# A bf16 copy of Wq and Wo in DRAM, made once at the start and read instead of casting loads

## The chip, the cores and the metric

One Trainium2 chip, one program on 8 cores. Each core works on its own half of one of four sequences and exchanges nothing with the others. The metric is device time in microseconds of the slowest core.

## What is computed

The reference is a transformer layer with a gate on its output: a layer norm, causal attention with 32 query heads and 8 key/value heads and a rotary embedding, and a low-rank mixture whose SiLU multiplies the attention's output.

```python
xn = _layernorm(x, axis=-1)                       # x: (4, 4096, 4096) float32
s = _L0_attn_ref(xn, Wq, Wk, Wv, Wo)              # q,k,v = xn @ W; rope; softmax(q k^T) v; out @ Wo
g = _silu(_L0_ffn_ref(xn, A, B, Wr, br))          # router softmax, low = xn A, out = low B * scores
x = x + s * g
return x
```

Wq and Wo are 4096 x 4096, Wk and Wv 4096 x 1024, all float32 in DRAM.

## The kernel before

The kernel keeps everything transposed: features on the partitions, 512 tokens across. It multiplies in bf16. Weights lie in DRAM in float32 and are converted by the DMA that loads them. Such a casting load is issued on POOL's queue (`load_wcol`, line 339): it brings one slab, 128 columns of a weight, into a tile of 128 x 4096 bf16 (1 MB). In DRAM a slab is 4096 runs of 512 bytes; in the tile each becomes 256 bytes.

There are two phases.

**First phase** (lines 470 to 566). Eight blocks of 512 tokens. For each, `p1_load` brings the 4 MB block of x (POOL's queue, casting, into XB0 or XB1 in turn) and `p1_stats` normalises it. Then for each of 8 key/value heads one slab of Wk and one of Wv are multiplied with the block (lines 496 and 535), K gets its rotary embedding, V is transposed, and both are stored to DRAM scratch (`kfs`, `vts`, on SP's queue). Two pairs of weight buffers take turns, so all 16 slabs of Wk and Wv are loaded again for every block.

**Second phase** (from line 570). Four slots of 512 query tokens, whose keys and values are 32, 24, 16 and 8 tiles long (`TRIPS`). In each slot:

- for each of 8 groups of four heads: four query projections (line 600, one slab of Wq each, 32 multiplications), the rotary embedding, norms for the softmax's bound, then the attention of the four heads (lines 697 to 747). Slab h+3 of Wq is loaded into one of three buffers wq0 to wq2 as soon as head h's projection is done (line 612). The keys and values of the next group come from kfs and vts on SP's queue (lines 678 and 681).
- the router and the low-rank gate (up to line 874),
- the output stage (lines 882 to 916): 32 chunks of 128 output features. Chunk `nck` multiplies its slab of Wo (three buffers, wo0 to wo2) with the attention's output: 32 multiplications, line 893. DVE multiplies the sum with the gate (line 908) and adds the residual tile xf (line 911), and SP stores it to `yqT` (line 914). The slab of chunk nck+3 is loaded when chunk nck is done (line 901). The residual tiles use two buffers, so the tile of chunk nck+1 (line 904) waits for the store of chunk nck-1.
- the setup of the next slot: sines, masks, its block of x, its layer norm.

The order on each engine is the order of the code. A small scheduler (`Sched`) works out for each instruction which semaphore counts it waits for, from the names of what it reads and writes. Every DMA takes the next of a fixed set of semaphore lanes, 4 on POOL and 6 on SP, and waits until that lane's last DMA has landed. So at most 4 DMAs of POOL and 6 of SP are in flight, and an engine that waits holds up all that stands behind it.

Of the kernel before, what the change touches and what calls it, by code (L numbers as in the profile page):

```python
# [11 lines left out]
BF16 = mybir.dt.bfloat16  # L12
# [9 lines left out]
NKV = 8  # L22
NH = 32
TW = 512
NTB = S // TW
NCD = D // 128
# [127 lines left out]
def build_program(dbg=False):  # L154
    nc = bass.Bass("TRN2", target_bir_lowering=False)
# [10 lines left out]
    Wq = din("Wq", [D, D])  # L166
    Wk = din("Wk", [D, KVD])
    Wv = din("Wv", [D, KVD])
    Wo = din("Wo", [D, D])
# [12 lines left out]
    constv = din("constv", [128, 12], F32)  # L182

    yqT = nc.dram_tensor("yqT", [D, NQ], F32, kind="ExternalOutput").ap()
    sk = "ExternalOutput" if dbg else "Internal"
    kfs = nc.dram_tensor("kfs", [NKV, 128, S], BF16, kind=sk).ap()
    vts = nc.dram_tensor("vts", [NKV, 128, S], BF16, kind=sk).ap()
# [11 lines left out]
    A = sch.add  # L199

    with ExitStack() as ctx:
        en = ctx.enter_context

        def sb(name, shape, dt):
# [15 lines left out]
        wq_sb = [sb(f"wq{i}", [128, NCD * 128], BF16) for i in range(3)]  # L220
        wo_sb = [sb(f"wo{i}", [128, NCD * 128], BF16) for i in range(3)]
# [78 lines left out]
                     writes=["cvt"], dma_sem="s_ld")  # L300
        for i, val in enumerate(CONST_VALS):
            nc.const_aps.register(F32, val, cvt[:, i:i + 1])
        for dst, nm, src in ((onec, "onec", ones_col), (oner, "oner", ones_row),
# [5 lines left out]
              writes=[nm], dma_sem="s_ld")  # L309
        A("gpsimd", lambda g: g.dma_start(  # L310
            out=a_sb[:].rearrange("p (c r) -> p c r", c=NCD),
            in_=Al.rearrange("(c p) r -> p c r", p=128)),
          writes=["a_sb"], dma_sem="s_cast")
        A("gpsimd", lambda g: g.dma_start(out=bm_sb[:], in_=Bml),
          writes=["bm_sb"], dma_sem="s_cast")

        A("tensor", lambda t: t.matmul(A0[:, 0:8], oner[:], brb[:], start=True, stop=True),
          reads=["oner", "brb"], writes=["A0"])
        A("vector", lambda v: v.tensor_copy(br_b[:], A0[:, 0:8]),
          reads=["A0"], writes=["br_b"])  # L320

        A("gpsimd", lambda g: g.dma_start(out=wr_bf, in_=Wr),
          writes=["XB0"], dma_sem="s_cast")
        for c in range(NCD):
# [3 lines left out]
              reads=["XB0", "idb"], writes=["D0"] if c == 0 else [])  # L328
        sch.mark_write("D0", "s_pe")
        A("vector", lambda v: v.tensor_copy(wrt[:], d0bf[:, 0:NCD * 8]),  # L330
          reads=["D0"], writes=["wrt"])

        def load_xblock(buf, bufname, src, col0):
            return A("gpsimd", lambda g: g.dma_start(
                out=buf[:].rearrange("p (c t) -> p c t", c=NCD),
                in_=src[:, col0:col0 + TW].rearrange("(c p) t -> p c t", p=128)),
                writes=[bufname], dma_sem="s_cast")

        def load_wcol(W, n0, buf, bufname):
            return A("gpsimd", lambda g: g.dma_start(  # L340
                out=buf[:].rearrange("p (c n) -> p c n", c=NCD),
                in_=W[:, n0:n0 + 128].rearrange("(c p) n -> p c n", p=128)),
                writes=[bufname], dma_sem="s_cast")

        def rep(ap2d, n, width):
            return ap2d.unsqueeze(1).to_broadcast([128, n, width])
# [111 lines left out]
        def p2_kv_load(slot):  # L458
# [5 lines left out]
                out=vtb[0][:, 0:T * 128], in_=vts[0][:, 0:T * 128]),  # L464
              reads=["vts.g0"], writes=[vtn[0]], dma_sem="s_ld")

        pending_vt = []
        p1_load(0)
        p1_stats(0)
# [4 lines left out]
        for tb in range(NTB):  # L474
# [4 lines left out]
            for g in range(NKV):  # L479
# [15 lines left out]
                for c in range(NCD):  # L495
# [4 lines left out]
                      reads=[wkn[gp], xname], writes=[PKn + ".lo"] if c == 0 else [])  # L500
                sch.mark_write(PKn + ".lo", "s_pe")
                A("vector", lambda v, gp=gp, PK=PK: v.tensor_copy(kraw[gp], PK[:, 0:512]),
                  reads=[PKn + ".lo"], writes=[krawn[gp]])
                A("tensor", lambda t, gp=gp, PK=PK: t.matmul(
                    PK[:, 512:1024], pib[:], kraw[gp], start=True, stop=True),
                  reads=[krawn[gp], "pib"], writes=[PKn + ".hi"])
                A("vector", lambda v, gp=gp, par=par: v.tensor_mul(
                    tmpA[:], kraw[gp], cosb[par][:]),
                  reads=[krawn[gp], f"cosb{par}"], writes=["tmpA"])
                A("vector", lambda v, par=par, PK=PK: v.tensor_mul(  # L510
                    tmpB[:], PK[:, 512:1024], sinb[par][:]),
                  reads=[PKn + ".hi", f"sinb{par}"], writes=["tmpB"])
                A("vector", lambda v, gp=gp: v.tensor_add(kout[gp], tmpA[:], tmpB[:]),
                  reads=["tmpA", "tmpB"], writes=[koutn[gp]])
                A("gpsimd", lambda gg, gp=gp: gg.tensor_mul(sqh, kout[gp], kout[gp]),
                  reads=[koutn[gp]], writes=["PP1.a"])
                A("tensor", lambda t: t.matmul(A0[0:1, :], onec[:], sqh,
                                               start=True, stop=True),
                  reads=["PP1.a", "onec"], writes=["A0"])
                if tb == 0:  # L520
                    A("vector", lambda v, g=g: v.reduce_max(
                        kmax2[0:1, g:g + 1], A0[0:1, :], axis=AX.X),
                      reads=["A0"], writes=["kmax2"])
                else:
                    A("vector", lambda v: v.reduce_max(sc1[:], A0[0:1, :], axis=AX.X),
                      reads=["A0"], writes=["sc1"])
# [38 lines left out]
        if dbg:  # L565
            A("sync", lambda s: s.dma_start(out=dkm, in_=kmax2[:]),
              reads=["kmax2"], dma_sem="s_st")
        p2_kv_load(0)

        for slot in range(NSLOT):  # L570
# [8 lines left out]
            for g in range(NKV):  # L579
# [14 lines left out]
                def proj(hl, g=g, xnb=xnb, xnname=xnname, projb=projb,  # L594
                         krs=krs, krn=krn, slot=slot):
                    h = 4 * g + hl
                    QB, QBn = projb[hl]
                    wqi = (slot * NH + h) % 3
                    for c in range(NCD):
                        A("tensor", lambda t, c=c, QB=QB, xnb=xnb, wqi=wqi: t.matmul(  # L600
                            QB[:], wq_sb[wqi][:, c * 128:(c + 1) * 128],
                            xnb[:, c * TW:(c + 1) * TW],
                            start=(c == 0), stop=(c == NCD - 1)),
                          reads=[f"wq{wqi}", xnname], writes=[QBn] if c == 0 else [])
                    sch.mark_write(QBn, "s_pe")
                    A("vector", lambda v, hl=hl, QB=QB, krs=krs: v.tensor_copy(
                        krs[hl], QB[:]),
                      reads=[QBn], writes=[krn[hl]])
                    nh = h + 3
                    if nh < NH or slot + 1 < NSLOT:  # L610
                        wqi2 = (slot * NH + nh) % 3
                        load_wcol(Wq, (nh % NH) * 128, wq_sb[wqi2], f"wq{wqi2}")

                def rot(hl, rotb=rotb, krs=krs, krn=krn, qbuf=qbuf,
                        qbname=qbname, spar=spar):
# [264 lines left out]
                      reads=[f"{xnname}.g{oc}"], dma_sem="s_st")  # L880

            for i3 in range(3):
                load_wcol(Wo, i3 * 128, wo_sb[i3], f"wo{i3}")
            A("sync", lambda s, q0=q0: s.dma_start(
                out=xf32[0][:], in_=xqT[0:128, q0:q0 + TW]),
              writes=["xf320"], dma_sem="s_ld")
            for nck in range(NCD):
                wp = nck % 2
                wb3 = nck % 3
                PB = pbigA if wp == 0 else pbigB  # L890
                PBn = "pbigA" if wp == 0 else "pbigB"
                for c in range(NCD):
                    A("tensor", lambda t, c=c, PB=PB, wb3=wb3, aob=aob: t.matmul(  # L893
                        PB[:, 0:512], wo_sb[wb3][:, c * 128:(c + 1) * 128],
                        aob[:, c * TW:(c + 1) * TW],
                        start=(c == 0), stop=(c == NCD - 1)),
                      reads=[f"wo{wb3}", f"{aoname}.h{c}"],
                      writes=[PBn + ".lo"] if c == 0 else [])
                sch.mark_write(PBn + ".lo", "s_pe")
                if nck + 3 < NCD:  # L900
                    load_wcol(Wo, (nck + 3) * 128, wo_sb[(nck + 3) % 3],
                              f"wo{(nck + 3) % 3}")
                if nck + 1 < NCD:
                    A("sync", lambda s, nck=nck, q0=q0: s.dma_start(
                        out=xf32[(nck + 1) % 2][:],
                        in_=xqT[(nck + 1) * 128:(nck + 2) * 128, q0:q0 + TW]),
                      writes=[f"xf32{(nck + 1) % 2}"], dma_sem="s_ld")
                A("vector", lambda v, nck=nck, PB=PB, xnb=xnb: v.tensor_tensor(
                    tmpc[:], PB[:, 0:512], xnb[:, nck * TW:(nck + 1) * TW], ALU.mult),
                  reads=[PBn + ".lo", f"{xnname}.g{nck}"], writes=["tmpA"])  # L910
                A("vector", lambda v, wp=wp: v.tensor_add(  # L911
                    xf32[wp][:], tmpc[:], xf32[wp][:]),
                  reads=["tmpA"], writes=[f"xf32{wp}"])
                A("sync", lambda s, nck=nck, q0=q0, wp=wp: s.dma_start(
                    out=yqT[nck * 128:(nck + 1) * 128, q0:q0 + TW], in_=xf32[wp][:]),
                  reads=[f"xf32{wp}"], dma_sem="s_st")
# [98 lines left out]
```

How the kernel before makes its waits and increments, by code:

```python
            def run(eng):  # L130
                waited = {}
                if name != "sync":
                    for (s, v) in preamble:
                        eng.wait_ge(sems[s], v)
                        waited[s] = v
                for w, fn, sem, amt in self.ev[name]:
                    for (s, v) in w:
                        if waited.get(s, 0) < v:
                            eng.wait_ge(sems[s], v)
                            waited[s] = v
                    ins = fn(eng)
                    if sem is not None:
                        assert ins is not None, f"event on {name} emitted nothing"
                        ins.then_inc(sems[sem], amt)
```

## Time and profile before

| what | value |
|---|---|
| median of 2 runs | 8021.4 us (8003.31 to 8039.5) |
| the profiled execution | 7996.54 us |
| its span on the slowest core (core 0) | 7994.9 us |
| spans of the 8 cores | 7877.3 to 7994.9 us |
| mean granted TensorE clock | 0.872 to 0.884 |
| PE busy | 6127.2 us (77%) |

The page's rows are from one profiled execution on its slowest core. In its slices each digit is the busy share of one fortieth of the span (200 us) in tenths. "DMA share" is the summed time of all transfers over 16 engines' time; transfers overlap within an engine, so it can pass 1. GB/s count the bytes as written, so a casting load reads twice what is counted.

### The profile page before, as it was taken

The numbers are of one execution on the slowest core, as the hardware profiler recorded it, in microseconds if no ns is written. First come the engines' busy times: TensorE is split into PE (matmuls) and PEld (weight loads), VectorE is DVE, ScalarE is ACT, GpSimd is POOL, SyncE is SP. The second block draws the span as 40 slices with busy tenths as digits, with TensorE's granted clock in tenths as the row PEclk, the third lists the DMA queues.
The fourth block names the chain that finished last, engine by engine and source line by source line (L and its number), as shares of the span: only waits on it lengthen the run. The fifth ranks groups of instructions, "written<-read, shape, count | busy, mean of one in ns | idle before, by whom it ended". The sixth has DMA issues, their size and how long they took to land.

```text
span 7994.9 us, 63595 instructions; the slowest of 8 cores (7877.3 to 7994.9 us)
## 1 busy us (share of the span) xinstructions
PE 6127.2 (77%) x23070; PEld 2131.7 (27%) x23070; DVE 1474.1 (18%) x2198; ACT 1918.3 (24%) x2176; POOL 886.2 (11%) x595
## 2 busy tenths in 40 slices
PE   4676676665999998865698989666898866588876
PEld 1222222222222222222222222222232222232222
DVE  1222212222111111100211121112211211222201
ACT  1000000000344443400243434101334310122210
POOL 1111111111000000011001010010100101011111
PEclk8888888887999999877799999887999988799988
DMA  9899999988442234299534254796443679666499
GB/s 109 95 95 93 97 117 105 99 89 94 61 46 32 32 41 39 26 108 104 85 39 48 35 56 37 72 127 95 53 44 45 57 72 124 92 62 57 48 103 131
DMA packets 1705814, 592.52 MB, mean 74 GB/s; under 512 B 1591709, under 2 KB 1664414, under 8 KB 1703326
## 3 DMA queue, kind: packets, MB, share of 16 engines
q0 software_dynamic: 1632640, 455.17, 61.9%
q1 hardware_dynamic: 72870, 133.28, 6.1%
q8 instruction: 193, 3.16, 0.2%
q14 instruction: 111, 0.91, 0.0%
HBM read 993.21 MB, written 50.33 MB: 131 GB/s over the span
## 4 chain that ended last, share of the span: by engine, by line
PE 59%; DMA 22%; DVE 9%; issue 5%; ACT 3%; another core or an unknown queue 1%; POOL 1%; SPq 0%; DVEq 0%; ACTq 0%; POOLq 0%
DMA yqT<-xf 13%; PE A L600 11%; PE A L743 5%; PE D L739 5%; PE D L747 5%; PE A L735 4%; PE pbigA L535 3%; PE pbigB L535 3%; DMA wo<-Wo 3%; PE pbigA L496 3%; PE pbigA L697 2%; PE pbigB L697 2%; PE pbigB L496 2%; DMA XB<-xqT 2%; PE pbigA L709 2%
## 5 line engine op out<-in xcount | busy, mean ns | idle before, releaser
L600 PE MATMUL A<-XB,wq 128*128 128x512 bf16 x4096 | 934.7, 389 | 98.0 <-DVE XB L419 55.0
L732 ACT ACTIVATE PP<-pbigA,negB 128x1024 bf16<-128x1024 f32 x640 | 713.0, 1114 | 632.7 <-PE pbigA L709 302.6
L732 ACT ACTIVATE PP<-pbigB,negB 128x1024 bf16<-128x1024 f32 x640 | 712.7, 1114 | 449.8 <-PE pbigB L714 244.0
L369 ACT ACTIVATE low_sb<-XB 128x512 bf16<-128x512 bf16 x192 | 120.0, 625 | 2896.3 <-DMA XB<-xqT 1498.9
L893 PE MATMUL pbigB<-XB,wo 128*128 128x512 bf16 x2048 | 537.8, 429 | 294.1 <-DMA wo<-Wo 201.2
L893 PE MATMUL pbigA<-XB,wo 128*128 128x512 bf16 x2048 | 528.5, 423 | 228.7 <-DMA wo<-Wo 151.2
L340 POOL DMA_DIRECT2D wq<-Wq x128 | 220.4, 1722 | 3286.9 <-PE A L600 2956.0
L600 PEld LDWEIGHTS A<-XB,wq 128*128 128x128 bf16 x4096 | 406.9, 100 | 607.1 <-issue 156.1
L735 PE MATMUL A<-PP,wkv 128*128 128x512 bf16 x1280 | 497.6, 389 | 67.2 <-ACT PP L732 40.9
L743 PE MATMUL A<-PP,wkv 128*128 128x512 bf16 x1280 | 508.0, 397 | 0.0
L753 DVE CAST XB<-A 128x512 bf16<-128x512 f32 x64 | 44.2, 691 | 2434.8 <-PE D L747 2415.7
L739 PE MATMUL D<-PP,onec 128*1 128x512 bf16 x1280 | 491.7, 384 | 0.0
L747 PE MATMUL D<-PP,onec 128*1 128x512 bf16 x1280 | 490.7, 383 | 0.0
L340 POOL DMA_DIRECT2D wo<-Wo x128 | 214.8, 1678 | 1800.5 <-PE pbigB L893 1192.7
L893 PEld LDWEIGHTS pbigB<-XB,wo 128*128 128x128 bf16 x2048 | 217.1, 108 | 613.1 <-issue 433.8
L893 PEld LDWEIGHTS pbigA<-XB,wo 128*128 128x128 bf16 x2048 | 215.1, 107 | 539.8 <-issue 355.1
L655 ACT ACTIVATE sc<-sc 1x1 f32<-1x1 f32 x32 | 6.5, 202 | 1420.1 <-DVE sc L652 1420.1
L496 PE MATMUL pbigA<-XB,wkv 128*128 128x512 bf16 x1024 | 241.3, 397 | 130.7 <-DMA wkv<-Wk 112.3
L375 PE MATMUL D<-XB,onec 128*1 128x512 bf16 x384 | 151.3, 394 | 207.8 <-DMA XB<-xqT 159.0
L911 DVE TENSOR_TENSOR xf<-tmpA,xf 128x512 f32<-128x512 f32 x128 | 88.6, 692 | 1194.5 <-DMA xf<-xqT 1193.0
L535 PE MATMUL pbigA<-XB,wkv 128*128 128x512 bf16 x1024 | 287.2, 451 | 0.0
L535 PE MATMUL pbigB<-XB,wkv 128*128 128x512 bf16 x1024 | 285.1, 448 | 0.0
(144 smaller groups left out, 5887.1 us busy)
## 6 DMA issues: line engine op xcount, KB each, us to landing
wq<-Wq POOLq DMA_DIRECT2D x128, 1024.0 KB, 12.5
wo<-Wo POOLq DMA_DIRECT2D x128, 1024.0 KB, 25.8
wkv<-Wk POOLq DMA_DIRECT2D x64, 1024.0 KB, 13.5
wkv<-Wv POOLq DMA_DIRECT2D x64, 1024.0 KB, 14.3
XB<-xT POOLq DMA_DIRECT2D x8, 4096.0 KB, 53.2
xf<-xqT SPq DMA_DIRECT2D x128, 256.0 KB, 11.3
yqT<-xf SPq DMA_DIRECT2D x128, 256.0 KB, 12.7
XB<-xqT POOLq DMA_DIRECT2D x4, 4096.0 KB, 37.1
```

The costliest lines, as they stand in the source:

```text
L340: return A("gpsimd", lambda g: g.dma_start(out=buf[:].rearrange("p (c n) -> p c n", c=NCD), in_=W[:, n0:n0 + 128].rearrange("(c p) n -> p ...
L496: A("tensor", lambda t, c=c, gp=gp, xbuf=xbuf, PK=PK: t.matmul(PK[:, 0:512], wk_sb[gp][:, c * 128:(c + 1) * 128], xbuf[:, c * TW:(c + 1) * ...
L535: A("tensor", lambda t, c=c, gp=gp, xbuf=xbuf, PV_=PV_: t.matmul(PV_[:, 0:512], wv_sb[gp][:, c * 128:(c + 1) * 128], xbuf[:, c * TW:(c + 1 ...
L600: A("tensor", lambda t, c=c, QB=QB, xnb=xnb, wqi=wqi: t.matmul(QB[:], wq_sb[wqi][:, c * 128:(c + 1) * 128], xnb[:, c * TW:(c + 1) * TW], s ...
L697: msk=msk: t.matmul(PB[:, 0:512], ksb[gp][:, kt * 128:(kt + 1) * 128], qbuf[:, la * TW:(la + 1) * TW], start=True, stop=not msk),
L709: msk=msk: t.matmul(PB[:, 512:1024], ksb[gp][:, kt * 128:(kt + 1) * 128], qbuf[:, lb * TW:(lb + 1) * TW], start=True, stop=not msk),
L732: A("scalar", lambda s, PB=PB, Pb=Pb, nbB=nbB: s.activation(Pb[:], PB[:], AF.Exp, bias=nbB[:, 0:1], scale=ISQ), reads=[PBn + ".lo", PBn + ...
L735: A("tensor", lambda t, kt=kt, Pb=Pb, gp=gp, T=T: t.matmul(A0[:], vtb[gp][:, kt * 128:(kt + 1) * 128], Pb[:, 0:512], start=(kt == 0), stop ...
L739: A("tensor", lambda t, kt=kt, Pb=Pb, T=T: t.matmul(D0[0:1, :], onec[:], Pb[:, 0:512], start=(kt == 0), stop=(kt == T - 1)), reads=["onec" ...
L743: A("tensor", lambda t, kt=kt, Pb=Pb, gp=gp, T=T: t.matmul(A1[:], vtb[gp][:, kt * 128:(kt + 1) * 128], Pb[:, 512:1024], start=(kt == 0), s ...
L747: A("tensor", lambda t, kt=kt, Pb=Pb, T=T: t.matmul(D1[0:1, :], onec[:], Pb[:, 512:1024], start=(kt == 0), stop=(kt == T - 1)), reads=["on ...
L893: A("tensor", lambda t, c=c, PB=PB, wb3=wb3, aob=aob: t.matmul(PB[:, 0:512], wo_sb[wb3][:, c * 128:(c + 1) * 128], aob[:, c * TW:(c + 1) * ...
```

## The change

Before anything else is loaded, but for the constants and the tables of the low-rank part, a new function `cache_weights` brings all 32 slabs of Wq and all 32 of Wo into SBUF with the casting load, through the six buffers wq0 to wq2 and wo0 to wo2 in turn, and SP stores each to a new DRAM tensor, `wqc` or `woc`, as 128 rows of 8 KB. In the second phase the casting loads of lines 612, 883 and 901 become plain loads of these copies (`load_wcached`) on SP's queue. The first three slabs of Wq for slot 0, issued at the end of the first phase, are still cast. `wkc` and `wvc` are declared and not used.

```diff
+    wqc = nc.dram_tensor("wqc", [NH, 128, NCD * 128], BF16, kind="Internal").ap()
+    woc = nc.dram_tensor("woc", [NH, 128, NCD * 128], BF16, kind="Internal").ap()
+    wkc = nc.dram_tensor("wkc", [NKV, 128, NCD * 128], BF16, kind="Internal").ap()
+    wvc = nc.dram_tensor("wvc", [NKV, 128, NCD * 128], BF16, kind="Internal").ap()
...
+        def cache_weights():
+            stage = [(wq_sb[i], f"wq{i}") for i in range(3)] + \
+                    [(wo_sb[i], f"wo{i}") for i in range(3)]
+            jobs = ([(Wq, wqc, n) for n in range(NH)]
+                    + [(Wo, woc, n) for n in range(NH)])
+            for i, (W, C, n) in enumerate(jobs):
+                buf, bname = stage[i % len(stage)]
+                A("gpsimd", lambda g, W=W, n=n, buf=buf: g.dma_start(
+                    out=buf[:].rearrange("p (c n) -> p c n", c=NCD),
+                    in_=W[:, n * 128:(n + 1) * 128].rearrange(
+                        "(c p) n -> p c n", p=128)),
+                  writes=[bname], dma_sem="s_cast")
+                A("sync", lambda s, C=C, n=n, buf=buf: s.dma_start(
+                    out=C[n], in_=buf[:]),
+                  reads=[bname], writes=[f"{CNAME[id(C)]}.{n}"], dma_sem="s_st")
...
+        def load_wcached(C, n, buf, bufname):
+            return A("sync", lambda s: s.dma_start(out=buf[:], in_=C[n]),
+                     reads=[f"{CNAME[id(C)]}.{n}"], writes=[bufname],
+                     dma_sem="s_ld")
...
+        cache_weights()
         pending_vt = []
         p1_load(0)
...
-                        load_wcol(Wq, (nh % NH) * 128, wq_sb[wqi2], f"wq{wqi2}")
+                        load_wcached(wqc, nh % NH, wq_sb[wqi2], f"wq{wqi2}")
...
-                load_wcol(Wo, i3 * 128, wo_sb[i3], f"wo{i3}")
+                load_wcached(woc, i3, wo_sb[i3], f"wo{i3}")
...
-                    load_wcol(Wo, (nck + 3) * 128, wo_sb[(nck + 3) % 3],
-                              f"wo{(nck + 3) % 3}")
+                    load_wcached(woc, nck + 3, wo_sb[(nck + 3) % 3],
+                                 f"wo{(nck + 3) % 3}")
```

How the instructions of POOL stand at the start of the program, before:

```order
L310 DMA a_sb<-Al 128x32x128
L314 DMA bm_sb<-Bml 128x4096
L322 DMA XB0<-Wr 8x4096
L334 DMA XB0<-xT 128x32x512
L340 DMA wkv0<-Wk 128x32x128
L340 DMA wkv1<-Wv 128x32x128
```

POOL at the same place after the change, with the first loads of the copy and its last ones:

```order
L314 DMA a_sb<-Al 128x32x128
L318 DMA bm_sb<-Bml 128x4096
L326 DMA XB0<-Wr 8x4096
L346 DMA wq0<-Wq 128x32x128
L346 DMA wq1<-Wq 128x32x128
...
L346 DMA wo0<-Wo 128x32x128
L356 DMA XB0<-xT 128x32x512
L362 DMA wkv0<-Wk 128x32x128
```

The first load of x, line 334 before and 356 after, now stands behind 64 casting loads.

SP in the output stage of slot 0, before:

```order
L884 DMA xf320<-xqT 128x512
L904 DMA xf321<-xqT 128x512
L914 DMA yqT<-xf320 128x512
L904 DMA xf320<-xqT 128x512
L914 DMA yqT<-xf321 128x512
```

SP at the same place after the change (xf320 and xf321 are the two residual buffers, wo0 and wo1 two of the slab buffers):

```order
L912 DMA xf320<-xqT 128x512
L368 DMA wo0<-woc 128x4096
L932 DMA xf321<-xqT 128x512
L942 DMA yqT<-xf320 128x512
L368 DMA wo1<-woc 128x4096
L932 DMA xf320<-xqT 128x512
L942 DMA yqT<-xf321 128x512
```

Each chunk's slab load now stands on SP's queue ahead of the next residual tile; before it stood on POOL's queue.

## Rows read from the trace of the kernel before

**Rows 1.** The page: its span, PE, and the slices of PE, DMA and GB/s

```profile
span 7994.9 us, 63595 instructions; the slowest of 8 cores (7877.3 to 7994.9 us)
...
PE   4676676665999998865698989666898866588876
...
DMA  9899999988442234299534254796443679666499
GB/s 109 95 95 93 97 117 105 99 89 94 61 46 32 32 41 39 26 108 104 85 39 48 35 56 37 72 127 95 53 44 45 57 72 124 92 62 57 48 103 131
```

**Rows 2.** The page: DMA queues (packets, bytes, share of 16 engines' span)

```profile
q0 software_dynamic: 1632640, 455.17, 61.9%
q1 hardware_dynamic: 72870, 133.28, 6.1%
```

**Rows 3.** The page: the chain that ended last, by line

```profile
DMA yqT<-xf 13%; PE A L600 11%; PE A L743 5%; PE D L739 5%; PE D L747 5%; PE A L735 4%; PE pbigA L535 3%; PE pbigB L535 3%; DMA wo<-Wo 3%; PE pbigA L496 3%; PE pbigA L697 2%; PE pbigB L697 2%; PE pbigB L496 2%; DMA XB<-xqT 2%; PE pbigA L709 2%
```

**Rows 4.** Stages: two of the first phase, then the four output stages

```profile
core 0: us, PE busy (x) PEld busy (x) DVE busy (x) ACT busy (x) POOL busy (x), PEclk, DMA share, GB/s
360.00:590.00 230.00, 156.09 (x610) 59.16 (x609) 58.51 (x73) 19.51 (x34) 36.94 (x25) 0.85 1.01 100
590.00:1740.00 1150.00, 781.10 (x3068) 296.81 (x3067) 288.01 (x357) 97.60 (x170) 178.69 (x121) 0.84 0.96 100
...
3381.80:3828.10 446.30, 279.35 (x1025) 111.07 (x1023) 42.88 (x62) 0.81 (x2) 48.59 (x29) 0.79 1.00 103
5061.00:5446.20 385.20, 265.22 (x1025) 108.07 (x1023) 42.88 (x62) 0.82 (x2) 48.61 (x29) 0.84 1.09 121
6457.20:6845.30 388.10, 262.29 (x1025) 107.31 (x1023) 42.89 (x62) 0.80 (x2) 48.60 (x29) 0.85 1.07 119
7621.00:7987.20 366.20, 256.10 (x1025) 105.28 (x1023) 42.19 (x61) 0.82 (x2) 48.62 (x29) 0.85 1.16 126
```

**Rows 5.** Waits in the last output stage, 7635 to 7995 us

```profile
DVE xf L911 <- DMA xf<-xqT: 281.3, 30, 17.0
...
PE pbigB L893 <- DMA wo<-Wo: 56.5, 10, 12.6
PE pbigA L893 <- DMA wo<-Wo: 48.0, 10, 15.7
```

**Rows 6.** PE in order of time in the last output stage

```profile
7855.53 7.07 PE L893 MATMUL pbigA<-XB,wo 128*128 128x512 bf16 x32
...
7890.29 9.76 PE L893 MATMUL pbigB<-XB,wo 128*128 128x512 bf16 x32 [3.45 <-DMA wo<-Wo]
```

**Rows 7.** DMA issues: count, size of one, median us to landing

```profile
wq<-Wq POOLq DMA_DIRECT2D x128, 1024.0 KB, 12.5
wo<-Wo POOLq DMA_DIRECT2D x128, 1024.0 KB, 25.8
...
xf<-xqT SPq DMA_DIRECT2D x128, 256.0 KB, 11.3
yqT<-xf SPq DMA_DIRECT2D x128, 256.0 KB, 12.7
...
kfs<-qpb SPq DMA_DIRECT2D x64, 128.0 KB, 2.8
```

**Rows 8.** POOL in order of time at the start

```profile
30.70 1.70 POOL L334 DMA_DIRECT2D XB<-xT  x1 [24.27 <-PE D L325]
```

**Rows 9.** Stretches of heavy DMA; columns as in rows 4

```profile
390.00:440.00 50.00, 27.70 (x107) 11.05 (x108) 8.12 (x14) 2.19 (x4) 10.54 (x7) 0.77 1.35 128
1080.00:1140.00 60.00, 31.86 (x119) 12.33 (x117) 8.64 (x15) 2.19 (x4) 7.18 (x5) 0.77 1.27 128
...
3200.00:3220.00 20.00, 14.11 (x41) 3.59 (x41) 5.20 (x11) 7.49 (x9) 7.55 (x5) 0.74 1.60 152
...
7940.00:7960.00 20.00, 14.59 (x60) 6.03 (x59) 2.77 (x4) 0.00 (x0) 3.35 (x2) 0.91 1.54 167
```

**Rows 10.** The load of K and V rows for one group, 1 MB each

```profile
2176.00:2184.00 8.00, 7.06 (x33) 3.16 (x33) 2.47 (x4) 3.77 (x6) 0.00 (x0) 1.00 0.85 246
```

**Rows 11.** Line 600: PE idle before it for a slab; one case

```profile
  DMA wq<-Wq: 16.6, 4
...
3187.96 9.15 PE L600 MATMUL A<-XB,wq 128*128 128x512 bf16 x32 [6.68 <-DMA wq<-Wq]
```

More of the change, by code:

```diff
@@ L331, in build_program @@
           reads=["D0"], writes=["wrt"])
+        CNAME = {id(wqc): "wqc", id(woc): "woc", id(wkc): "wkc", id(wvc): "wvc"}
+        def cache_weights():
[13 more added lines that the diff above has]
+                  reads=[bname], writes=[f"{CNAME[id(C)]}.{n}"], dma_sem="s_st")
         def load_xblock(buf, bufname, src, col0):
```

## The prediction

> **What bounds the kernel now.** I read the page from the top. Its first rows [rows 1] show an execution in two halves. PE is busy for 77% of the span, and the digits say where it isn't: the first ten slices (some 2000 us, the K and V projection) and every later place where PE falls to 6 to 8 and the DMA digit rises. In the first ten slices the DMA digit is 8 or 9 throughout, at 93 to 117 GB/s. The page's chain of waits [rows 3] then names the other places: 13% of the span is `yqT<-xf` and 3% `wo<-Wo`, both of the output stage (line 893), against 11% for the query projection of line 600. A table of stages [rows 4] gives that stage's length in the four slots, from its first multiplication to its last: 446.3, 385.2, 388.1 and 366.2 us, together 1585.8 us. Each has 1024 multiplications in 32 chunks. PE is at work for 256 to 279 us of each, at a mean clock of 0.79 to 0.85.
>
> The row of one undisturbed chunk says what the stage would need: 32 multiplications take 7.07 us at the full clock, the higher of its two levels (2.4 GHz), and 9.76 us where PE had stood still for 3.45 us before a weight load landed and then began at 1.2 GHz [rows 6]. At 7.07 us the stage would last 226 us. What it waits for is in its waits [rows 5]: PE for `wo<-Wo`, 56.5 and 48.0 us in the last slot, and DVE 281.3 us for the residual tile xf. Both are transfers. `wo<-Wo` takes 25.8 us from issue to landing, xf 11.3 and yqT 12.7, where a store of 128 KB, half their size, takes 2.8 [rows 7]. So the chunk waits for congested DMA engines. The casting loads congest them: the software queue carries 455.17 MB in 61.9% of the span, the hardware queue 133.28 MB in 6.1% [rows 2].
>
> **Two prices per megabyte.** 61.9% of 7994.9 us is 4949 us for 455.17 MB, so one slab of 1.049 MB (128 columns of a weight, 4096 runs of 256 bytes written) costs 11.4 us of all 16 engines when these do one transfer each at a time. On the hardware queue 6.1% is 488 us for 133.28 MB, so the same megabyte costs 3.84 us. The engines' share of a stretch may pass 1, since transfers overlap. The heaviest 50 and 60 us of the first phase stand at 1.35 and 1.27, the heaviest 20 us windows at 1.60 with casting loads alone (152 GB/s) and at 1.54 with output traffic beside them (167 GB/s) [rows 9].
>
> **Term 1, the copy ahead of everything.** It adds 64 casting loads on POOL's queue and 64 stores on SP's, and the order shows that all 64 loads stand ahead of the first load of x, on which all other work hangs. Nothing computes meanwhile: PE has only the 32 small transposes of the router weight. One slab is 11.4 + 3.84 = 15.2 us of engine time. I divide by a share of 1.35, that of the heavier stretch of rows 9 which is longer than 20 us, because four casting loads may be in flight (four semaphore lanes) with the stores on another queue, so the engines never lack work: 15.2 / 1.35 = 11.3 us, and 64 of them 723 us. SP's waits don't slow this: slab i needs the buffer of slab i-6, which leaves its store five slabs (56 us) of room. A little is won at the start, since POOL now needn't wait until 30.70 us for PE before its next issue [rows 8]; the two table loads have the engines until then, so I take off only 3 us. **Term 1: +720 us.** Bounds: share 1.60 gives 9.5 us and 608 less 3 = 605 us; share 1.0, which the first phase shows over long stretches (1.01 and 0.96 in rows 4), gives 975 less 3 = 972 us. I keep the heavy value since in those long stretches the next load waits for PE to free its buffer, which nothing does here.
>
> The trace shows over the whole span no rate near that of the copy. One page has a price for it: the Trainium skill, HBM Reference, Specifications (TRN2), puts a core's share of its HBM at about 358 GB/s when both cores of a pair stream. A slab of the copy reads 2.10 MB and writes 1.05 MB there, an estimate of 8.8 us by that page, 563 us in all, which would make the sum 157 us smaller; my row-based term lies above that floor. The casting burst of rows 9 reads twice what it writes, 304 GB/s, which agrees with the limit but doesn't test it with stores.
>
> **Term 2, the output stage.** A chunk now moves a cached slab (1.05 MB in 8 KB rows), an xf tile and a yqT tile (0.26 MB each), all on the hardware queue: 1.57 MB, which at 133.28 MB in 488 us is 5.8 us at a share of 1. The nearest transfer of that kind, the pair of K and V rows, ran at 246 GB/s and a share of 0.85 [rows 10]: 6.4 us. Both are under PE's 7.07 us but not by much. The issue order changes too: SP carries the slab load, which waits for PE to end the chunk, ahead of the next xf load, which waits for the yqT store two chunks back. Behind the waiting slab load stand xf and yqT, and DVE waits for xf. A xf load issued right behind a slab lands some 2 + 4.3 + 1.1 = 7.4 us later (2 us as the fixed part of the 2.8 us store, then slab and tile at 246 GB/s). It is wanted 7 to 8 us after its issue, so this just fits. I take 7.5 us a chunk, 240 us a stage: 7.07 where all fits, with a few waits in between and the slow start. Four stages: 1585.8 - 960 = 626. **Term 2: -626 us.** Bounds: 226 us + 4 for start and end, four times 230, gives -666; 9.5 us a chunk, half way between PE's rows of 9.15 and 9.76 after a wait, gives 304 us a stage and -370.
>
> A rule that bears on how close this is: the Trainium skill, DMA: Bandwidth & Descriptors, Specifications, gives 435 GB/s as the fabric's ceiling. By it a chunk's 1.57 MB would take 3.6 us, an estimate, and only PE's 7.07 us would be left; the sum would be 40 us smaller. The row of 246 GB/s at a share of 0.85 is well below, and I go by the row.
>
> **Term 3, the projections.** 125 of the 128 slabs of Wq come from the copy too (the first three are still cast, at the end of the first phase). PE waited for them only 16.6 us, four times [rows 11], with some 2 us of slow clock behind each (9.15 against 7.07 us [rows 6, 11]): 25 us are gone. In every other group the slab landed in time, since the attention of the group hides it, so halving its 12.5 us buys nothing. The K and V rows of the next group are now issued behind the fourth slab of a group instead of before the first: a group's attention (40 us or more) still lies ahead of their use, so this costs nothing; without that cover it would be 10 us a group. **Term 3: -25 us.** A gain from POOL no longer writing descriptors between its squares lies between 0 and 1.7 us a group; I count none.
>
> **Not touched.** The first phase keeps its casts of Wk and Wv (two of the four new DRAM tensors are never used), so its 2000 us only start later. The x loads between slots stay.
>
> **The sum.** 720 - 626 - 25 = +69 us. The profiled execution took 7996.5 us and would take 8066; it lies 25 us under the median of the two runs, 8021.4. Against the median the forecast is 8021 + 69 = **8090 us**, 0.9% slower. A measurement of this kernel tells about 2% (160 us) from no change, so that is within what counts as the same.
>
> **The rivals.**
> - **The copy doesn't overlap (slower).** Place: the stretch before the first x load. If the engines run at a share of 1.0, as over the long stretches of the first phase, it costs 972 us; with terms 2 and 3 as above that is 8021 + 972 - 651 = 8342 us. It decides from 811 us, that is 12.7 us a slab or a share under 1.20. For it: no row of 100 us or more stands above 1.16, and that one is an output stage, in which loads also wait for buffers. Against it: in those rows something always waited. 22%.
> - **The xf and yqT loop keeps the chunk (slower).** DVE's wait of 281.3 us says that xf, not the weight, came last as often as not. With two xf buffers, two chunks last at least one load, one store and two DVE operations. At today's 11.3 + 12.7 + 1.4 = 25.4 us that would be 12.7 us a chunk, and nothing at all would be gained (8021 + 720 - 25 = 8716). But today's latencies are queueing; behind a 4.3 us slab they come to 7 to 8 us each, 8 to 9 us a chunk. With PE falling to its lower clock at each wait, 9.5 us a chunk: 8021 + 720 - 370 - 25 = 8346 us. 10%.
> - **Stores in the shade of the casts (faster).** If casts run at the 152 GB/s of rows 9 (6.9 us a slab, 442 us) and the stores cost nothing beside them, with stages of 230 us: 8021 + 442 - 666 - 25 = 7772 us. For it: that burst. Against it: it lasted 20 us with share 1.60, which leaves no room for 64 MB more. By rows I give it 10%. By the HBM page's 358 GB/s it could not happen, since 3.15 MB in 6.9 us is 456 GB/s; no run here shows that limit yet.
> - **That it doesn't do what it says.** Each cached load stands in the order after its store, and both read the bf16 values that the cast made, so the slabs are the same; I see no way for this one beyond the 25 us of term 3 not coming.
>
> **How the numbers follow.** Forecast 58%, no overlap 22%, loop 10%, shade 10%. Faster by over 2%: 0.10; slower: 0.22 + 0.10 less a little, as each reaches down to the limit, 0.30; the same: 0.60. The forecast's own range runs from 605 us of copy with stages of 230 us (8021 + 605 - 666 - 25 = 7935) to 811 us of copy (8181). The range that holds 8 in 10 leaves out most of the fast case and the ends of the slow ones: 7900 to 8330.
>
> **What would show it.** The first x load should be issued some 700 us after the start, with no PE before it, a DMA share near 1.35 and near 185 GB/s moved until then. Line 893's stages should last 230 to 260 us with a clock of 0.9 or more, DVE's wait for xf should fall from 281 us to a few tens of us a stage, `wo` should have no wait over 5 us, and PE's four waits for wq should be gone. The first phase should keep its 2000 us. I am wrong if the copy takes under 600 or over 810 us, or if the stage stays above 290 us.

## The result, and the profile after

The changed kernel is slower. Its profiled execution took 8313.9 us (before: 7996.5), and over the repeated runs the ratio to the kernel before is 1.037, with a 95% interval of 1.027 to 1.048. The forecast was 1.009 (8090 against 8021 us); applied to 8021 us, the measured ratio gives some 8320. Executions in which the cores of one die ran at a lower clock than the other die's are left out wherever whole times are compared.

The page of the changed kernel, the lines that answer to [rows 1] and [rows 3], with the clock's slices besides:

```profile
span 8312.3 us, 63926 instructions; the slowest of 8 cores (8122.6 to 8312.3 us)
...
PE   0000046676667589989989698998968888968889
...
PEclk9999998888888789999999899999989999989989
DMA  9999999999999850110005301111631110531117
GB/s 122 131 128 134 125 123 99 98 98 91 97 103 105 99 88 31 36 56 31 31 37 187 102 33 51 38 46 37 183 101 51 51 51 37 198 86 64 56 44 217
...
PE A L628 11%; PE pbigA L921 5%; PE pbigB L921 5%; PE A L771 5%; PE D L775 5%; PE D L767 5%; PE A L763 4%; PE pbigA L563 3%; PE pbigB L563 3%; PE pbigA L524 3%; PE pbigA L725 2%; PE pbigB L725 2%; DMA XB<-xqT 2%; PE pbigB L524 2%
```

Five slices of PE are 0: the copy. After it comes the first phase as it was, and then slots in which the DMA digit is mostly 0 or 1, where it was 2 to 9. `yqT<-xf`, 13% of the chain before, is gone from it.

The same in microseconds, on core 0 of both. The marks are the first starts of PE's lines in order of time; an output stage ends with its last multiplication, any other part where the next begins.

| part | before | after | difference |
|---|---|---|---|
| start to the first statistics multiplication | 78.7 | 1104.9 | +1026.2 |
| first phase, to the first query projection | 1931.4 | 1926.3 | -5.1 |
| slot 0 to its output stage | 1371.7 | 1361.4 | -10.3 |
| slots 1 to 3 to theirs | 3019.5 | 3027.1 | +7.6 |
| four output stages | 1585.9 | 888.0 | -697.9 |
| end | 7.7 | 4.6 | -3.1 |
| span | 7994.9 | 8312.3 | +317.4 |

Core 0 had the longest output stages of all eight cores before: the four together take 1459 to 1586 us, 1528 in the median, and 888 on every core after. So the saving is 698 us on core 0 and 640 in the median.

The two large entries, first the copy. PE's longest wait, the casting queue's landings and the engines in the copy's middle (columns of the last row as in [rows 4]):

```profile
PE D L402 <- DMA XB<-xT: 1076.8, 1, 1076.8
```

```profile
wq<-Wq POOLq DMA_DIRECT2D x20, 1024.0 KB, 48.6
wqc<-wq SPq DMA_DIRECT2D x17, 1024.0 KB, 15.9
```

```profile
130.00:430.00 300.00, 0.00 (x0) 0.00 (x0) 0.00 (x0) 0.00 (x0) 31.84 (x19) 1.00 1.05 135
```

PE has nothing at all in these 300 us, POOL issues 19 slabs, and the DMA share is 1.05 where I had counted on 1.35. A slab costs 16.0 us (1026 / 64) on core 0 and 15.8 in the median of the cores (1013 / 64), whose first statistics multiplications start at 1008 to 1114 us.

The four output stages, which answer to the last four of [rows 4]:

```profile
4392.60:4615.00 222.40, 221.94 (x1025) 100.31 (x1023) 43.22 (x63) 0.79 (x2) 0.00 (x0) 1.00 0.65 211
5850.00:6073.00 223.00, 222.07 (x1025) 100.31 (x1023) 43.58 (x63) 0.96 (x2) 0.26 (x1) 1.00 0.76 210
7085.00:7308.00 223.00, 222.39 (x1025) 100.37 (x1024) 43.38 (x63) 1.08 (x2) 0.00 (x0) 0.99 0.61 210
8085.40:8307.70 222.30, 222.30 (x1025) 100.43 (x1025) 42.86 (x62) 1.14 (x2) 0.00 (x0) 1.00 0.77 211
```

The stages last 222 us whatever the slot (the windows are up to 1 us wider); PE never stops and has the full clock. 211 GB/s move at a share of only 0.61 to 0.77. What waited in [rows 5] no longer does; DVE in the last stage now has

```profile
DVE tmpA L936 <- PE pbigA L921: 109.8, 16, 31.2
...
DVE xf L939 <- DMA xf<-xqT: 3.4, 6, 0.8
```

and the landings that answer to [rows 7] are

```profile
wo<-woc SPq DMA_DIRECT2D x128, 1024.0 KB, 6.4
wq<-wqc SPq DMA_DIRECT2D x125, 1024.0 KB, 4.8
...
xf<-xqT SPq DMA_DIRECT2D x128, 256.0 KB, 5.3
yqT<-xf SPq DMA_DIRECT2D x128, 256.0 KB, 6.3
```

PE in order of time shows a chunk at its floor:

```profile
8203.95 7.07 PE L921 MATMUL pbigB<-XB,wo 128*128 128x512 bf16 x32
8210.86 7.07 PE L921 MATMUL pbigA<-XB,wo 128*128 128x512 bf16 x32
```

From start to start it is 6.91 us: a row of 7.07 us overlaps the next by 0.16.

So on core 0 the saving was underestimated by 72 us and the copy by 306, and the question for the experiments is why a slab of the copy took 16 us.

### The profile page after: what moved, and what is told of

Read it like the earlier page. It is cut to its first block, busy times and chain, and to the rows that moved or that the text cites. A ratio compares the mean times of both kernels' runs of the same rounds, so it can differ in the third digit from the quotient of the medians.

```text
span 8312.3 us, 63926 instructions; the slowest of 8 cores (8122.6 to 8312.3 us)
## 1 busy us (share of the span) xinstructions
PE 5954.8 (72%) x23070; PEld 2101.5 (25%) x23070; DVE 1474.0 (18%) x2198; ACT 1916.9 (23%) x2176; POOL 564.3 (7%) x406
## 4 chain that ended last, share of the span: by engine, by line
PE 65%; another core or an unknown queue 14%; DVE 8%; issue 4%; DMA 4%; ACT 3%; POOL 1%; DVEq 0%; ACTq 0%; POOLq 0%
PE A L628 11%; PE pbigA L921 5%; PE pbigB L921 5%; PE A L771 5%; PE D L775 5%; PE D L767 5%; PE A L763 4%; PE pbigA L563 3%; PE pbigB L563 3%; PE pbigA L524 3%; PE pbigA L725 2%; PE pbigB L725 2%; DMA XB<-xqT 2%; PE pbigB L524 2%
## 5 line engine op out<-in xcount | busy, mean ns | idle before, releaser
L760 ACT ACTIVATE PP<-pbigA,negB 128x1024 bf16<-128x1024 f32 x640 | 713.0, 1114 | 632.8 <-PE pbigA L737 305.8
L921 PE MATMUL pbigA<-XB,wo 128*128 128x512 bf16 x2048 | 455.8, 381 | 0.0
L921 PE MATMUL pbigB<-XB,wo 128*128 128x512 bf16 x2048 | 452.5, 379 | 0.0
L657 POOL TENSOR_TENSOR PP<-qpb 128x512 bf16<-128x512 bf16 x128 | 146.6, 1145 | 3694.8 <-PE A L628 2768.5
L402 PEld LDWEIGHTS D<-XB,onec 128*1 128x1 bf16 x384 | 32.0, 83 | 1252.9 <-issue 1248.6
L725 PE MATMUL pbigA<-qpb,wkv 128*128 128x512 bf16 x640 | 262.6, 410 | 0.0
## 6 DMA issues: line engine op xcount, KB each, us to landing
wq<-Wq POOLq DMA_DIRECT2D x20, 1024.0 KB, 48.6
```

The source lines that it names most:

```text
L402: A("tensor", lambda t, c2=c2: t.matmul(D0[0:1, :], onec[:], xbuf[:, c2 * TW:(c2 + 1) * TW], start=(c2 == 0), stop=(c2 == NCD - 1)), reads ...
L657: A("gpsimd", lambda gg, hl=hl, qbuf=qbuf, krs=krs: gg.tensor_mul(krs[hl], qbuf[:, hl * TW:(hl + 1) * TW], qbuf[:, hl * TW:(hl + 1) * TW]) ...
L725: msk=msk: t.matmul(PB[:, 0:512], ksb[gp][:, kt * 128:(kt + 1) * 128], qbuf[:, la * TW:(la + 1) * TW], start=True, stop=not msk),
L760: A("scalar", lambda s, PB=PB, Pb=Pb, nbB=nbB: s.activation(Pb[:], PB[:], AF.Exp, bias=nbB[:, 0:1], scale=ISQ), reads=[PBn + ".lo", PBn + ...
```

## The experiments

Four things could explain it: the stores; the casts themselves, by where they read; too few transfers in flight; or simply that engine time adds up. In all runs the mark is the start of the first statistics multiplication, before which only the copy stands, but for what takes 79 us without a copy. So a slab's time is the mark less 79 us, over the number of slabs. "Median" is over the eight cores.

**Casts without stores.** The second phase loads by casting, as before.

```diff
-                A("sync", lambda s, C=C, n=n, buf=buf: s.dma_start(
-                    out=C[n], in_=buf[:]),
-                  reads=[bname], writes=[f"{CNAME[id(C)]}.{n}"], dma_sem="s_st")
```

> The copy's 64 casting loads without its 64 stores; the second phase loads by casting, as before the change. Read: when PE's first statistics multiplication (line 402) starts; 78.7 us before the change, 1104.9 with it (1026 us more, 16.0 us a slab, DMA share 1.03). Theory 'stores disturb the casts': alone they run as in the burst of the trace before (share 1.35 to 1.6), 7.2 to 8.5 us a slab, first multiplication at 540 to 620 us. Theory 'transfer times just add, at a share near 1': 11.4 us a slab, 800 us. Theory 'casts are slow by themselves when all eight cores make them at once': 13 us a slab or more, 900 us or later, share near 1 or below.

Measured: 778 to 870 us, median 841, 11.9 us a slab. On the slowest core:

```profile
130.00:430.00 300.00, 0.00 (x0) 0.00 (x0) 0.00 (x0) 0.00 (x0) 39.55 (x24) 1.00 1.05 84
```

The stores are not it: without them the share is still 1.05 and only 84 GB/s move. The time lies between the last two of the expectation's theories (800 us, and 900 or later), so this run alone doesn't tell whether the source, the transfers in flight or engine time that adds up sets the 11.9 us.

**The same number of casts, from Wk and Wv.**

```diff
-            jobs = ([(Wq, wqc, n) for n in range(NH)]
-                    + [(Wo, woc, n) for n in range(NH)])
+            jobs = ([(Wk, wqc, n % NKV) for n in range(NH)]
+                    + [(Wv, woc, n % NKV) for n in range(NH)])
```

> As the casts alone, but the 64 slabs come from Wk and Wv (rows 4 KB apart, each slab eight times over eight... each of the 8 slabs four times) instead of Wq and Wo (rows 16 KB apart). Theory 'the wide row pitch of Wq and Wo slows the reads': over 10% less time per slab than in the run with Wq and Wo. Theory 'contention or engine time, whatever the source': within 5% of that run.

Measured: 587 to 627 us, median 619, 8.4 us a slab:

```profile
130.00:430.00 300.00, 0.00 (x0) 0.00 (x0) 0.00 (x0) 0.00 (x0) 57.87 (x35) 1.00 1.43 122
```

Same bytes, same runs of 512 bytes, same buffers, and the share is 1.43. The source matters by 30%. But this run differs in two things: rows 4 KB apart instead of 16 (the pitch, the distance in DRAM from one row of the weight to the next), and few slabs read again and again.

**Few slabs, but of Wq and Wo** (`n % NKV` on Wq and Wo).

> Casts alone again, from Wq and Wo (rows 16 KB apart), but only slabs 0 to 7 of each, four times over, as the run with Wk and Wv had it. That run took 8.6 us a slab on core 0 (first statistics multiplication at 626 us, share 1.4), the one with all slabs of Wq and Wo 11 to 12.4 us (778 to 870 us, share 1.0 to 1.1). Theory 'row pitch': as with all slabs of Wq and Wo, 780 to 870 us. Theory 'reading the same 8 slabs again is what was quick': 590 to 640 us.

Measured: 794 to 873 us, median 825, 11.7 us a slab:

```profile
130.00:430.00 300.00, 0.00 (x0) 0.00 (x0) 0.00 (x0) 0.00 (x0) 43.58 (x26) 1.00 1.10 91
```

Reading the same slabs again doesn't help. What is left is the pitch.

**All slabs of Wq and Wo, with rows 20 KB apart.** Each row of the two weights in DRAM gets 1024 unused columns.

```diff
-    Wq = din("Wq", [D, D])
+    Wq = din("Wq", [D, D + 1024])
...
-        "Wq": np.ascontiguousarray(np.asarray(Wq_, np.float32)),
+        "Wq": np.pad(np.asarray(Wq_, np.float32), ((0, 0), (0, 1024))),
```

(and so for Wo)

> Casts alone of all slabs of Wq and Wo, with the two weights laid out in DRAM with rows 20 KB apart (1024 unused columns behind each row) instead of 16 KB. Theory 'the 16 KB pitch, a large power of two, makes rows fall on the same part of the memory': 8 to 9.5 us a slab, first statistics multiplication at 590 to 690 us, share 1.3 or more. Theory 'any far row is slow' (contention of the eight cores over far-apart reads): 770 us or later, as with 16 KB.

Measured: 606 to 652 us, median 629, 8.6 us a slab:

```profile
130.00:430.00 300.00, 0.00 (x0) 0.00 (x0) 0.00 (x0) 0.00 (x0) 56.98 (x34) 1.00 1.39 120
```

Rows farther apart than before, and as quick as those of Wk and Wv. So it is not that rows lie far apart: of the three pitches measured, 4, 16 and 20 KB, only 16 KB is slow. In engine time the four runs differ little: a slab's time on the core of the window, times its share, is 12.2 us at 4 KB, 12.1 at 20 KB, and 13.0 and 12.9 at 16 KB. What falls at 16 KB is how far the transfers overlap: the share goes from about 1.4 to 1.05 and 1.10.

The Trainium skill, DMA: Bandwidth & Descriptors, Latency and other measured facts, tells of a like effect for plain copies: they slow down at row pitches that are large powers of two, from 512 KB up, and 4 KB more a row bring back the full rate; it calls the mechanism an inference. These runs agree with it at 16 KB against 20 KB, a smaller pitch than any listed there. That 4 KB, a power of two as well, is quick shows that here it takes more than a power of two. None of them shows the mechanism.

**The stores alone.** Six slabs are cast and all 64 stores kept; most copies hold wrong slabs.

> Only the first six slabs are cast and all 64 stores of 1 MB are kept, so most copies hold wrong slabs: the stretch is read, not the output. Theory 'times just add': stores alone take 2.8 to 3.8 us each, 64 in 180 to 250 us, share 0.7 to 1. Theory 'stores are the slow part' (writing DRAM beside reading it): 5 us or more each, over 320 us. The second phase with its output stages of 228 us should stay as in the changed kernel, so the span should be about 7995 - 626 - 25 plus 50 to 300 us, 7400 to 7650 us.

Contrary to what the expectation says of the second phase, this kernel still cast its weights there, so that sentence had nothing to test. A store's issue to landing, and the engines between casts and x load:

```profile
wqc<-wq SPq DMA_DIRECT2D x17, 1024.0 KB, 21.6
```

```profile
90.00:200.00 110.00, 0.00 (x0) 0.00 (x0) 0.00 (x0) 0.00 (x0) 6.70 (x4) 1.00 1.06 239
```

With six in flight, 21.6 us to landing are 3.6 us a store, within the 2.8 to 3.8 expected. In the copy a store adds 3.9 us to a cast at the 16 KB pitch (15.8 - 11.9). My price of 3.84 us was about right; that it would be partly hidden was not, at that pitch.

**More transfers in flight.**

```diff
-             "gpsimd": tuple(f"gl{i}" for i in range(4))}
+             "gpsimd": tuple(f"gl{i}" for i in range(8))}
```

> The changed kernel with 8 instead of 4 semaphore lanes for POOL's DMAs. In the copy three casts were in flight at a time. Theory 'too few in flight': with more lanes the slab gets cheaper by over 1 us, first statistics multiplication under 1040 us. Theory 'the engines and the memory set the pace, or the queue's own space': within 20 us of 1105 on core 0 and of 1092 in the median of cores.

Measured: 1092 to 1139 us, median 1101 (1092 with 4 lanes), core 0 at 1128, 3 us later than either theory allowed. On the slowest core, core 1, a landing and what POOL waited for during the copy:

```profile
wq<-Wq POOLq DMA_DIRECT2D x20, 1024.0 KB, 50.2
```

```profile
POOL wo L346 <- issue: 481.9, 31, 33.6
```

A slab's `wq<-Wq` lands after 50.2 us, three times the 16 to 17 us of a slab: three casts were in flight with 4 lanes (48.6 us) and still are with 8. With 8 lanes POOL's idle time before a cast has no releaser that the profile shows ("issue"), so something other than a lane or a buffer ends the number; what, stays open. The theory falls as far as lanes are concerned.

**The change with the padded layout.** The step that puts the pieces together.

> The changed kernel with the rows of Wq and Wo 20 KB apart in DRAM. The casts alone fell from 11.9 to 8.6 us a slab (median of cores) with that layout, and the stores came to 3.9 us a slab (15.8 less 11.9). If store time simply adds to cast time: 12.5 us a slab, first statistics multiplication at about 78 + 64 x 12.5 = 880 us. If stores and casts overlap once the pitch is right, as the forecast had it with a share of 1.35: 11.3 us, 800 us or earlier. The rest as in the changed kernel, so a span of 8312 less 220 to 300: 8010 to 8090 us.

Measured: 768 to 813 us, median 798, 11.25 us a slab, span 7983.5 us. The middle of the copy, and PE's wait, on the slowest core:

```profile
130.00:430.00 300.00, 0.00 (x0) 0.00 (x0) 0.00 (x0) 0.00 (x0) 43.58 (x26) 1.00 1.26 183
```

```profile
PE D L402 <- DMA XB<-xT: 784.1, 1, 784.1
```

294 us of the copy's 1013 were the pitch (median 1092 against 798). Stores now cost 2.65 us beside a cast (11.25 - 8.6) instead of 3.9, so store and cast do overlap once the engines aren't held up. The kernel then stands at its time before (7985.0 us in its one run, against 7996.6 to 8114.1 of the kernel before beside it).

**The kernel before, padded.**

> The kernel before, with only the rows of Wq and Wo 20 KB apart. With the padded casts alone the output stages took 349, 304, 308 and 314 us instead of 446, 385, 388 and 366, so 310 us should go: 7690 us in the profile, 4% faster. If the gain in that run came from something else (other phase of the cores against each other), it would be under 150 us.

Measured: 7662.0 us span, 7663.5 and 7729.5 us; ratio to before 0.956, interval 0.938 to 0.975. Its output stages:

```profile
3366.00:3729.00 363.00, 270.77 (x1026) 109.23 (x1025) 43.62 (x64) 1.25 (x3) 48.92 (x30) 0.84 1.22 128
4961.00:5265.00 304.00, 242.28 (x1025) 102.12 (x1024) 43.44 (x63) 1.07 (x2) 48.59 (x29) 0.94 1.30 153
6275.00:6590.00 315.00, 251.24 (x1025) 104.83 (x1022) 43.36 (x63) 0.71 (x2) 48.60 (x29) 0.89 1.26 148
7367.00:7657.00 290.00, 239.14 (x1026) 102.27 (x1025) 43.55 (x63) 1.20 (x2) 48.59 (x29) 0.94 1.33 159
```

Shares of 1.22 to 1.33 stand where [rows 4] had 1.00 to 1.16. Together the stages take 1268 us on this slowest core against 1586 on the slowest before, and 1241 against 1528 in the median of the cores. So a good part of what the change took out of them, 287 of 640 us in the median, was the pitch, not the cast or its bytes.

**Half the copy** (Wo only; Wq is cast in the slots as before).

> Half the copy: only the 32 slabs of Wo, Wq is loaded by casting again. Every theory in which a slab has one price says 32 slabs fewer at 16.0 us, so first statistics multiplication at 78.7 + 513 = 592 us, output stages of 228 us as in the changed kernel, the projections' 25 us back: span 8312 - 513 + 25 = 7824 us, 2% faster than before the change. If the price per slab came from a fixed part of the copy, or if the cached Wq mattered more than 25 us, it would be above 7900 us.

Measured: median 583 us to the mark (504 / 32 = 15.8 us a slab again), span 7887.6 us, four runs at 7830.7 to 7889.1 beside one of 8057.6 for the kernel before. Slot 0's output stage and the copy on the slowest core:

```profile
130.00:430.00 300.00, 0.00 (x0) 0.00 (x0) 0.00 (x0) 0.00 (x0) 30.16 (x18) 1.00 1.04 131
3964.00:4186.50 222.50, 222.39 (x1026) 100.52 (x1025) 42.92 (x62) 1.27 (x3) 0.00 (x0) 1.00 0.72 210
```

The price per slab is one number, and the copy of Wq was a loss by itself: some 510 us for next to nothing.

**The copy in slot 0.** `cache_weights` goes; each slab of Wq is stored when slot 0 has cast it anyway, and Wo is cast and stored beside slot 0's attention.

```diff
-        cache_weights()
...
+                        if slot == 0 and nh < NH:
+                            load_wcol(Wq, nh * 128, wq_sb[wqi2], f"wq{wqi2}")
+                            store_copy(wqc, nh, wq_sb[wqi2], f"wq{wqi2}")
...
+                if slot == 0:
+                    for n in range(4 * g, 4 * g + 4):
+                        load_wcol(Wo, n * 128, wo_sb[n % 3], f"wo{n % 3}")
+                        store_copy(woc, n, wo_sb[n % 3], f"wo{n % 3}")
```

> The same copies, made in slot 0 of the second phase: each slab of Wq is stored when slot 0 has loaded it anyway, and the 32 slabs of Wo are cast and stored during slot 0's attention, four per group. Nothing stands before the first x load. If the copy's price was only its place on the path, 1026 us go and the output stages of 228 us stay: 7995 - (1585.8 - 4 x 228) - 20 plus 0 to 60 us for DMA work beside slot 0's attention, 7300 to 7380 us in the profile. If the copy slows slot 0 (PE waits for wq behind it), slot 0 gains up to 16 us a group, 7450 us.

Measured: span 7390.6 us; ratio to before 0.919, interval 0.911 to 0.928. Slot 0 up to its output stage, and what PE waits for in it on the slowest core:

```profile
2031.00:3481.00 1450.00, 1255.92 (x4482) 391.39 (x4571) 187.07 (x333) 632.02 (x632) 137.04 (x93) 0.92 0.69 107
```

```profile
PE pbigB L658 <- POOL PP L651: 56.6, 16, 11.4
PE A L618 <- DMA wq<-Wq: 50.3, 7, 20.4
```

The same two waits in slot 0 of the kernel before, on core 0:

```profile
PE pbigB L636 <- POOL PP L629: 33.9, 16, 2.9
PE A L600 <- DMA wq<-Wq: 12.2, 2, 6.7
```

In slot 0 the DMA share is 0.69. Before, the longest stretch of it had 0.31 (core 0 of the kernel before):

```profile
2040.00:3160.00 1120.00, 1039.39 (x3813) 320.71 (x3812) 148.92 (x263) 534.15 (x517) 72.85 (x51) 0.96 0.31 37
```

So most of the copy fits into idle DMA time, but not all: slot 0 takes 1450 us on this core (1364 before on the same core) and, core for core, 7 to 86 us more than before, 29 in the median. The two waits above are 61 us longer than before. The span is 11 us over the 7380 that was expected. This version beats both kernels.

**The same with the padded layout.**

> The copy in slot 0 with the padded layout. Slot 0 took 1450 us with the copy in it against 1372 before the change (78 us more), the other slots and the output stages (222 us) were as in the changed kernel. If those 78 us come from slow casts ahead of the Wq slabs, most go: 7310 to 7350 us in the profile. If they come from SP and POOL waiting in line for each other, they stay: 7380 to 7400 us.

Measured: 7294.3 us in one run. On core 4 of the profile slot 0 took 1378 us, and PE waited 14.9 us for wq and 36.9 for POOL's squares; on cores 4 to 7 slot 0 took 1365 to 1378 us against 1371 to 1418 unpadded. That speaks for slow casts ahead of the Wq slabs; with one run, and cores that differ by 79 us in the unpadded version, it is not shown.

**Also Wk and Wv.** Block 0 of the first phase stores its slabs, blocks 1 to 7 load the copies on SP's queue.

> As the copy in slot 0, and also Wk and Wv: block 0 of the first phase casts their slabs and stores each, blocks 1 to 7 load the copies on SP's queue. If the first phase is held by its casting loads, its seven blocks go from 229 us towards 175 to 195 us, 250 to 380 us less than the run before: 6950 to 7100 us. If PE and the chain of rotary, squares and norms set its pace and only the waits for slabs go (112 us), some 7200 us.

Measured: 7244.2 and 7351.4 us. The first phase on core 2 (second row: the same core before):

```profile
70.00:1855.00 1785.00, 1274.15 (x4978) 486.20 (x5074) 488.88 (x584) 178.86 (x307) 108.89 (x89) 0.86 0.51 116
```

```profile
79.00:1986.00 1907.00, 1287.15 (x4980) 489.61 (x5075) 488.09 (x584) 177.34 (x307) 296.84 (x201) 0.84 0.93 100
```

The DMA share falls from 0.93 to 0.51 and the phase only by 122 us on this core, and by 73 in the median of the cores (1905 to 1832 us). PE's wait for Wk slabs before, on core 0, was of that size:

```profile
PE pbigA L496 <- DMA wkv<-Wk: 112.3, 6, 25.2
```

So the first phase, whose DMA digits were 8 and 9, was held by its transfers only at these few waits, and the second theory fits. On cores 0 and 1 of the profile the phase even took 1906 and 1909 us, at a granted clock of 0.78 against 0.86 on core 2; why these had the lower clock is open.

## Why the prediction was wrong

**Term 1, the copy, failed; it alone made the prediction wrong.** The step is "I divide by a share of 1.35". The division of engine time was right in kind, and the 15.2 us of engine time a slab were nearly right (16.0 us at a share of 1.05 are 16.8). But the share, 1.35, was taken from a stretch of the first phase, whose slabs come from Wk and Wv with rows 4 KB apart, and used for slabs of Wq and Wo with rows 16 KB apart. At 4 and 20 KB casts alone reach 1.4 in long stretches, at 16 KB 1.05 to 1.10. As built the term is 1013 us in the median and 1026 on core 0, where 720 were forecast and over 810 was named as the sign of being wrong. With the padded layout it measures 720 us (798.4 - 78.7). That this meets the forecast to the microsecond is luck: on the slowest core the share was 1.26 and not 1.35, and a slab's engine time 14.5 us (11.5 x 1.26) and not 15.2, two errors that largely cancel. The premise that four casts are in flight was off too: three were. The row that warned of a lower share was quoted: the output stages, the only long stretches with casts from Wo, stood at 1.00 to 1.16 [rows 4], and I put that down to loads that wait for their buffers. The padded kernel before, at 1.22 to 1.33, shows that much of it was the pitch. The reason given against the low share, that in the first phase a load waits for PE to free its buffer, was right for slabs of Wk and Wv: without that wait they reach 1.43. The upper bound, a share of 1.0 and 972 us, fell short too, as it took a cast's own time, 11.4 us, from the mean over all sources; at the 16 KB pitch it was some 13.

**The rival "the copy doesn't overlap" is what happened**, in its place and above its price: it decides from 811 us, and 1013 were measured. I had given it 22%. Its reason was only half there. Stores add 3.9 us in full, but the larger part is that the casts themselves don't overlap among each other at this pitch.

**Term 2, the output stages, right in mechanism, 72 us short in size on core 0.** Measured -698 us against -626 and a bound of -666. Part of that is the choice of core 0, which had the longest stages before; in the median of the cores the saving is 640. The rest, and the fall of the bound, comes from the chunk: its floor was read as 7.07 us, the length of a row, where start to start is 6.91. The waits I allowed for didn't come: the xf tile landed in 5.3 us rather than 7.4, and SP's new order, a slab load ahead of each xf load, cost nothing. The rival of the xf and yqT loop falls with this: its latencies of 11.3 and 12.7 us went to 5.3 and 6.3 once the casts were gone. DVE's 281.3 us (3.4 after) had read like a bound of its own, but it was the casts' congestion seen from another engine.

**Term 3, the projections, came to -3 us instead of -25**: 10 us less in slot 0, 8 more in the others. PE's waits for wq are gone from its list, and slot 0 has 10 of its 12 us of them back. In the later slots PE's wait for the x load grew instead, from 159.0 to 166.9 us over the four slots, and ate the rest. A gain from POOL's missing descriptors isn't to be seen, as counted.

**"Not touched"** held: the first phase 1926 against 1931 us. One reading was off, without bearing on the sum: the first ten slices move 89 to 117 GB/s, not 93 to 117.

**The rival "stores in the shade"** falls: even padded, a store adds 2.65 us. The 358 GB/s that the Trainium skill, HBM Reference, Specifications (TRN2), gives a core was not what set the copy's pace: even the padded copy moves only 3.15 MB a slab in 11.25 us, 280 GB/s. Nor do the runs show it as a bound over short stretches. For 20 us of an x load between two slots, core 5 of the padded change wrote 203 GB/s by casting loads alone, so it read 406:

```profile
2520.00:2540.00 20.00, 0.00 (x0) 0.00 (x0) 0.00 (x0) 0.00 (x0) 1.69 (x1) 0.50 1.34 203
```

The figure is stated for both cores of a pair streaming, and what the other core moved just then isn't known. The 435 GB/s of the Trainium skill, DMA: Bandwidth & Descriptors, Specifications, was not put to the test.

Open: why the 16 KB pitch costs anything, and whether it needs all eight cores at once. One burst, a slab of Wq and three of Wo, ran at a share of 1.60 [rows 9] at this pitch, in the middle of a slot, where in the casts alone no 20 us of the copy on the slowest core passed 1.31. That fits a collision between cores which read alike at the same time, but no run separated the cores.

## What to carry to other kernels

Make a copy of reused weights where the DMA engines have nothing to do, not ahead of the first work: the same copy cost 1013 us at the start and 7 to 86 us, by core, beside attention. Price a transfer by rows with the same source layout, its row pitch among them, not only by rows with the same size of run. When several engines wait for transfers in one stage, ask first whether one class of transfers congests them all.

## What the runs showed of the hardware

- Casting loads of 512-byte runs, all eight cores at once: 8.4 us per MB written at a pitch of 4 KB, 8.6 at 20 KB, 11.7 and 11.9 at 16 KB.
- Padding Wq and Wo alone, with no other change, made the kernel 4.4% faster (interval 2.5 to 6.2%).
- Taking nearly half of the DMA load out of the first phase (share 0.93 to 0.51 on core 2) shortened it by 6% there and by 4% in the median of the cores: a DMA digit of 9 did not mean that the transfers set the pace.
- A stage whose transfers no longer made PE wait ran at a granted clock of 0.99 to 1.00, the higher level throughout, where it had 0.79 to 0.85 before.
